# Weighted values in one run, and layer 1 in steps of two key chunks: a two-layer gated cross-attention kernel on one core

## The reference, cut to what matters

```python
x = x + tanh(g_xattn[0]) * L0_xattn(layernorm(x), ctx, ctx)      # two softmaxes, a1 - lam * a2
x = x + tanh(g_ffn[0]) * L0_ffn(layernorm(x))
x = x + tanh(g_xattn[1]) * L1_xattn(layernorm(x), ctx, ctx, mask)
x = x + tanh(g_ffn[1]) * L1_ffn(layernorm(x))
# in either attention, for every batch row and head:
scores = q @ k.T / sqrt(hd);  out = softmax(scores) @ v
```

## Time and profile before

| | us |
|---|---|
| median of 3 runs (2351.14 to 2353.91) | 2351.37 |
| the profiled execution, its own time | 2361.65 |
| its span from first to last instruction | 2359.2 |

### The profile page before, as it was taken

The page is one execution under the profiler, slowest core; times in us unless marked ns, Lnnn a source line. Parts: engine busy times, 40 slices in busy tenths (PEclk is TensorE's granted clock), DMA queues, the critical chain, the costliest instruction groups (busy, mean ns, idle before and its releaser), DMA issues. The chain is left out here.

```text
span 2359.2 us, 67435 instructions
## 1 busy us (share of the span) xinstructions
PE 2192.7 (93%) x27256; PEld 1303.0 (55%) x27256; DVE 1677.1 (71%) x3697; ACT 1507.8 (64%) x2133; POOL 1278.9 (54%) x1418
## 2 busy tenths in 40 slices
PE   4799999999999999999967957999999999999798
PEld 3255555555555555555536843666655666666576
DVE  3688888888888888888816555777766677774644
ACT  2177788777877778778763322767666667766322
POOL 5335655655654554655333445777766777762232
PEclk8599999999999999999997975999999999999699
DMA  3635344344444444444201027667665666661100
GB/s 105 128 77 113 96 98 109 101 94 108 106 97 99 112 96 95 115 93 94 48 7 57 24 61 149 137 142 137 143 131 120 127 144 140 138 126 24 54 1 16
DMA packets 113421, 227.82 MB, mean 97 GB/s; under 512 B 46052, under 2 KB 58596, under 8 KB 112612
## 3 DMA queue, kind: packets, MB, share of 16 engines
q1 hardware_dynamic: 113124, 223.67, 42.8%
HBM read 146.77 MB, written 76.48 MB: 95 GB/s over the span
## 5 line engine op out<-in xcount | busy, mean ns | idle before, releaser
L1061 ACT ACTIVATE probs<-score_ps 125x896 f32<-125x896 f32 x1152 | 1014.3, 915 | 210.3 <-PE score_ps L954 207.9
L1119 DVE TENSOR_REDUCE max_part<-max_ps 112x1 f32<-112x500 f32 x1024 | 654.7, 668 | 115.3 <-PE spare_ps L923 68.3
L970 PE MATMUL acc_ps<-probs,vext 125*32 125x224 f32 (+1 forms) x12288 | 673.2, 316 | 6.6 <-issue 6.1
L923 PE MATMUL max_ps<-kstack,qstack 48*112 48x500 f16 x1535 | 508.1, 405 | 4.9 <-DVE max_part L1119 2.6
L954 PE MATMUL score_ps<-qstack,kstack 50*125 50x224 f16 (+1 forms) x6144 | 454.8, 244 | 17.2 <-ACT probs L1061 13.9
L954 PEld LDWEIGHTS score_ps<-qstack,kstack 50*125 50x125 f16 x6144 | 344.4, 134 | 183.8 <-issue 122.2
L1116 DVE CUSTOM_DVE_ANT_0 kstack<-max_ps,kstack 112x500 f32<-112x500 f32 x511 | 335.3, 675 | 134.2 <-PE max_ps L923 80.1
L1119 DVE TENSOR_REDUCE max_part<-spare_ps 112x1 f32<-112x500 f32 x512 | 343.3, 670 | 64.6 <-PE max_ps L923 63.5
L970 PEld LDWEIGHTS acc_ps<-probs,vext 125*32 125x32 f32 x12288 | 261.7, 109 | 225.8 <-issue 156.5
L923 PE MATMUL spare_ps<-kstack,qstack 48*112 48x500 f16 x769 | 310.7, 404 | 20.2 <-issue 16.9
L923 PEld LDWEIGHTS max_ps<-kstack,qstack 48*112 48x112 f16 x1535 | 173.5, 129 | 143.4 <-issue 77.7
(11 more groups left out here) (200 smaller groups left out, 2697.8 us busy)
## 6 DMA issues: line engine op xcount, KB each, us to landing
kstack<-k_parts SPq DMA_DIRECT2D x384, 187.5 KB, 6.6
k_parts<-khl SPq DMA_DIRECT2D x128, 375.0 KB, 2.8
ctx_f<-in_ctx SPq DMA_DIRECT2D x32, 750.0 KB
ctx_f<-context_parts SPq DMA_DIRECT2D x32, 750.0 KB, 4.4
context_parts<-ctx_f SPq DMA_DIRECT2D x16, 750.0 KB, 3.8
context_parts<-kstack SPq DMA_DIRECT2D x16, 750.0 KB, 3.5
mask_in<-in_mask SPq DMA_DIRECT2D x128, 82.0 KB
qrows<-q_parts SPq DMA_DIRECT2D x384, 7.0 KB, 7.0
```

What stands on the lines that cost most here:

```text
L923: nc.tensor.matmul(room(("P", n, p))[0:PIECE, 0:TK], qstack[n % SLOTS][rows, c, PIECE * i:PIECE * (i + 1)], kstack[n % SLOTS][rows, c, TK ...
L970: last = nc.tensor.matmul(acc_ps[32 * j:32 * j + 32, TT * S * i:TT * S * (i + 1)].rearrange("p (s c) -> p s c", s=S), vext[n % SLOTS][:, t ...
L1061: nc.scalar.activation(probs[t % 2][:, 896 * h:896 * h + 896].rearrange("k (b c) -> k b c", b=2), score_ps[(t * H + h) % 2][0:KT, :, 0:448 ...
L1119: nc.vector.reduce_max(best, scores, AX.X).then_inc(s_red, 1)
```

## The change

Five things change, all in `attend`.

1. `weigh` has no index i: its products follow one another in one run. In layer 0 that is 8 products; before, the search's second pair and the preparation stood between the groups of four (except in step 0).
2. A layer-1 step is now two chunks: `L.steps` is 6 there, `STEPS` replaces `NKT`. A step has two score parts in both layers, in layer 1 one for each chunk, and `weigh` covers both (16 products). `AHEAD` is 3 of 6 steps in layer 1, so the search of row n+2 begins in step 3 of row n; four pieces go in each step.
3. In layer 1 the preparation moves from the search banks to the score banks, and `where` is rewritten: a pair is now (step, bank of the pair). K 0, 1, 2 stand in steps 3, 4, 4, V in 1, 2, 5, M in 3, A in 5, and F is one use of four turned blocks and not two of two.
4. Where the step before had a preparation in the score banks ("crowded"), the second score part stands behind `weigh` (`LATE_SECOND`); otherwise the two parts stand together at the step's head. The first part waits, as layer 0's did, for both exponentials of the step before; a layer-1 chunk waited only for the exponential two chunks back.
5. On SP, in layer 1, `next_context` moves from before `fill_m` to behind `store_k`.

```diff
         keyed = [(kind, i) for kind in "TK" for i in range(NTHIRD)]
     else:
-        where = {("V", 0): (0, 2), ("F", 0): (1, 2), ("V", 1): (2, 2), ("F", 1): (3, 2), ("V", 2): (4, 2), ("K", 0): (5, 2),
-                 ("K", 1): (6, 2), ("M", 0): (7, 2), ("K", 2): (8, 2), ("A", 0): (10, 2)}
+        where = {("F", 0): (1, 1), ("V", 0): (1, 0), ("V", 1): (2, 0), ("M", 0): (3, 1), ("K", 0): (3, 0),
+                 ("K", 1): (4, 0), ("K", 2): (4, 1), ("A", 0): (5, 1), ("V", 2): (5, 0)}
...
-    assert per_step * NKT == L.pieces
-    AHEAD = 5
+    per_step = L.pieces // STEPS
+    assert per_step * STEPS == L.pieces
+    AHEAD = 3 if L.masked else 5
     early = AHEAD * per_step
+    LATE_SECOND = True
```

```diff
@@ -721,8 +718,6 @@
                 if n + 3 < B:
                     load_q(n + 3)
                     next_mask(n + 3)
-                    if L.masked:
-                        next_context(n + 4)
                 if n + 3 < B and not L.masked:
                     next_context(n + 4)
                     store_context(n + 3)
@@ -730,6 +725,8 @@
                     fill_m(n + 1)
                 if n + 3 < B:
                     store_k(n + 3)
+                    if L.masked:
+                        next_context(n + 4)
         s_chain = sem(L.name + "_normalisation_chain")
```

```diff
-                step = n * NKT + t
-                number = step * H + place
+                step = n * STEPS + t
+                number = step * 2 + place
                 h = halves_of(step)[place]
-                if L.masked:
-                    at_least(pe, s_exp, number - 1)
-                elif place == 0:
+                if place == 0:
                     at_least(pe, s_exp, number)
                 else:
...
                     if L.masked:
                         pe.wait_ge(s_big, n + 1)
-                buf = score_ps[(t * H + h) % 2]
-                keys = slice(KT * t, KT * t + KT)
+                buf = score_ps[h]
+                chunk, columns = (t, range(h * 2, h * 2 + 2)) if H == 2 else (2 * t + h, range(PAIRS))
+                keys = slice(KT * chunk, KT * chunk + KT)
...
+            def weigh(n, t):
+
+                pe.wait_ge(s_exp, (n * STEPS + t + 1) * 2)
+                if t == 0:
+                    at_least(pe, s_os, n)
+                    pe.wait_ge(s_v, NTHIRD * (n + 1))
+                chunks = [(t, 0)] if H == 2 else [(2 * t + h, 896 * h) for h in range(2)]
+                for chunk, column in chunks:
+                    for i in range(2):
+                        for j in range(4):
+                            u = 4 * i + j
+                            moving = probs[t % 2][:, column:column + S * 896].rearrange("k (s c) -> k s c", s=S)[:, :, TT * u:TT * u + TT]
+                            last = nc.tensor.matmul(
+                                acc_ps[32 * j:32 * j + 32, TT * S * i:TT * S * (i + 1)].rearrange("p (s c) -> p s c", s=S),
+                                vext[n % SLOTS][:, chunk, u, :], moving, start=(chunk == 0 and i == 0), stop=(chunk == NKT - 1),
+                                skip_group_check=True)
+                last.then_inc(s_av, 1)
```

```diff
-                for t in range(NKT):
+                for t in range(STEPS):
                     weighed = (n, t - 1) if t else (n - 1, LAST)
+                    crowded = n * STEPS + t - 1 in in_scores.values()
                     scores(n, t, 0)
+                    if not crowded:
+                        scores(n, t, 1)
                     search(searched(n, t, 0))
-                    if H == 2:
+                    if crowded and not LATE_SECOND:
                         scores(n, t, 1)
-                    for i in range(2):
-                        if i == 1 and (t or H == 1):
-                            search(searched(n, t, 1))
-                            for user in at_step(n, t, 1):
-                                use(user)
-                        if weighed[0] >= 0:
-                            weigh(*weighed, i)
-                    if t == 0 and H == 2:
-                        search(searched(n, t, 1))
-                    for user in at_step(n, t, 2):
+                    if weighed[0] >= 0:
+                        weigh(*weighed)
+                    if crowded and LATE_SECOND:
+                        scores(n, t, 1)
+                    search(searched(n, t, 1))
+                    for user in at_step(n, t):
                         use(user)
```

```diff
+                    dst, part = (turned[:, i, :], spare_ps[0:SQ, :]) if H == 2 else (
+                        turned[:, :, 0:256], spare_ps[0:SQ, :].rearrange("q (i x) -> q i x", i=2))
+                    nc.scalar.activation(dst, part, ACT.Copy).then_inc(s_turned, 1)
```

More of the change, by code:

```diff
@@ L63, in __init__ @@
         self.o_cols = self.cols // 4
-        self.uses_f = 2
+        self.uses_f = self.halves
+        self.steps = NKT if self.halves == 2 else NKT // 2
 L0 = Layer("L0", 32, 4, False)
@@ L575, in attend, with at_step @@
     LEAD = {"T": 3, "K": 3, "V": 2, "M": 1, "F": -1, "A": -1}
-    def at_step(n, t, side):
-        return [(kind, n + LEAD[kind], i) for (kind, i), place in where.items()
-                if place == (t, side) and 0 <= n + LEAD[kind] < B]
+    def at_step(n, t):
+        return [(kind, n + LEAD[kind], i) for (kind, i), (step, _) in where.items()
+                if step == t and 0 <= n + LEAD[kind] < B]
     def searched(n, t, k):
-        if 2 * k >= per_step:
-            return []
-        d, place = (1, early + t * per_step) if t < NKT - AHEAD else (2, (t - NKT + AHEAD) * per_step)
+        d, place = (1, early + t * per_step) if t < STEPS - AHEAD else (2, (t - STEPS + AHEAD) * per_step)
         return [("P", n + d, place + 2 * k + r) for r in range(2)] if n + d < B else []
@@ L592, in attend @@
     for n in range(B):
-        for t in range(NKT):
-            middle, last = at_step(n, t, 1), at_step(n, t, 2)
-            spare_uses += middle + last
-            if H == 2:
-                in_scores.update({user: n * NKT + t for user in middle})
-                middle = []
-            order += searched(n, t, 0) + middle + searched(n, t, 1) + last
+        for t in range(STEPS):
+            spare_uses += at_step(n, t)
+            in_scores.update({user: n * STEPS + t for user in at_step(n, t)})
+            order += searched(n, t, 0) + searched(n, t, 1)
     order += [(kind, B - 1, i) for kind, i in turnaround]
@@ L904, in use @@
                     pe.wait_ge(s_os, n + 1)
-                    for b in range(2 * S):
-                        k = (i * 2 * S + b) * SQ
+                    for b in range(4):
+                        k = (i * 4 + b) * SQ
                         last = nc.tensor.transpose(spare_ps[0:SQ, 128 * b:128 * b + 128], out_sb[:, k:k + SQ], ident[:, :])
@@ L949, in scores @@
                                          big_eye[HALF * r:HALF * r + SQ, :], start=True, stop=False, skip_group_check=True)
-                here = PAIRS // H
-                for k in range(here):
+                for k, c in enumerate(columns):
                     for r in range(2):
                         rows = slice(HALF * r, HALF * r + KROWS + 2)
-                        last = nc.tensor.matmul(buf[0:KT, r, GC * k:GC * (k + 1)], kstack[n % SLOTS][rows, h * here + k, keys],
-                                                qstack[n % SLOTS][rows, h * here + k, :], start=not L.masked, stop=True,
+                        last = nc.tensor.matmul(buf[0:KT, r, GC * k:GC * (k + 1)], kstack[n % SLOTS][rows, c, keys],
+                                                qstack[n % SLOTS][rows, c, :], start=not L.masked, stop=True,
@@ L1070, in _ @@
             for n in range(B):
-                for t in range(NKT):
-                    for h in range(H):
-                        exps(n, t, h)
+                for t in range(STEPS):
+                    for place in range(2):
+                        exps(n, t, place)
                     if t == 0 and n:
                         copy_output(n)
-                    for user in at_step(n, t, 1) + at_step(n, t, 2):
+                    for user in at_step(n, t):
                         drain(user)
@@ L1150, in _ @@
             for n in range(B):
-                for t in range(NKT):
+                for t in range(STEPS):
                     for user in searched(n, t, 0):
                         reduce_piece(user)
-                    for user in at_step(n, t, 1):
-                        drain(user)
-                    if t == where["F", 1][0] + 1 and n:
+                    if t == where["F", L.uses_f - 1][0] + 1 and n:
                         reciprocals(n)
```

57 lines of the change are left out of this document (19 added, 38 removed).

## The result

The changed kernel takes **2452.56 us** (median; 2446.73 to 2465.94) against 2352.64 us before: 4.3% slower, ratio 1.0429, 95% interval 1.0377 to 1.048. The forecast was 2445. The profiled execution took 2446.73 us, with a span of 2444.9 (2359.2 before).

A forecast was written before the change was run, and what follows sets the result against it. TensorE's order was taken to bound the kernel, and after the change the keys' circle in layer 1. From 2361.65 us, -24 + 110 + 2 gave 2450, taken as 2445; its own range 2400 to 2495, for all 2335 to 2500.

The forecast's parts named there:

- Layer 0, -24 us: In layer 0's attention, a row was to take 34.2 us against 35.01, -24 us over 29 rows.
- The chain that was said to set the step: In layer 0, late second scores, their exponential, then the next step's first scores: a step lasts at least 2.84 us.
- TensorE alone, 21.0: In layer 1, a row whose keys come in time was to take 21.0 us, 1.3 less than before.
- The circle, 23.6: In layer 1, from a row's first search piece through key projection, split, store and fill to the next: 23.6 us.
- X to S: In layer 1, from the first search piece (X) to the end of GpSimd's last key split (S): 10.4 us.
- The context ahead of the fill, 1.6: In layer 1, the context's load stands before the keys' fill in SP's order and delays it: 1.6 us, 0 to 2.5.
- The slow clock, 1.6: In layer 1, TensorE's wait for the fill brings its clock down: 1.6 us a circle, 0 to 2.9.
- The mean: In layer 1, the circle with context and slow clock was to last 26.8 us a row, +110 us over 29 rows.
- S to the next X: In layer 1, from the last key split's end to the next first search piece: 13.2 us and 1.6 for the context.
- the +88 of the sum: Whole kernel against the profiled execution before: -24 in layer 0, +110 in layer 1, +2 for the last rows.

The follow-up runs named there:

- repaired kernel: The changed kernel with layer 1's keys half a step earlier, the context's load ahead of the maxima's fill, and the search half a step later: 2322.87 us.
- experiment 5: The changed kernel with eighteen products that nobody reads before each row's first search piece in layer 1: 2439.86 us.
- experiment 4: The changed kernel with layer 1's context load behind the fill and the queries, one turn of the loop later: 2437.48 us.
- the first edit of experiment 6: The changed kernel with layer 1's key projections half a step earlier in TensorE's order, the context's load not moved: 2477.22 us.

## Why the prediction was right

- **Layer 0, -24 us.** Right: 34.11 a row for 34.2, and -23 us by itself. The chain that was said to set the step also gives 3.66 for the 3.67 of the kernel without the run. The prediction did not see that, with the preparation at the step's end, the late second part also hides the read-out of the bank; without that the row is 36.71.
- **TensorE alone, 21.0.** Right: 20.79 with a small fill, 21.0 in the repaired kernel.
- **The circle, 23.6.** Right in kind, shown by taking out the fill's bytes (wait gone) and by moving either end. With the clock up X to S is 10.37 (experiment 5). The terms that the prediction lists add up to 10.3, not to the 10.4 that it writes.
- **The context ahead of the fill, 1.6.** Right: the fill lands at S + 14.7 in the median for 14.8, and at S + 13.1 with the context behind it (13.2 predicted). The two share the queue: in 1595.5 to 1598 and 1598.5 to 1603 the DMA share was 0.96 and 1.06, at 292 and 226 GB/s, where the fill alone moves 111. By the rule of the Trainium skill that the prediction named (DMA: Bandwidth & Descriptors, Queues, rings and completion order) a ring is consumed in ring order. The trace agrees, with a fill that comes later by the load ahead of it. Sharing the bandwidth without any order could delay it too, and no run here tells the two apart.
- **The slow clock, 1.6.** Somewhat small: X to S is 12.5 for 10.37 with the clock up, so 2.1. The stall that the prediction read as 2.2 us stands as 1.98 in the earlier trace rows.
- **The mean.** 26.65 for 26.8, and here luck had a part: X to S is half a us longer than the 12.0 counted, S to the next X half a us shorter on average than 14.8. The stretch grew by 105 for 110.
- **The rest.** From layer 0's stretch to layer 1's are 350.0 us, 344.7 before. Of these 5 us, 3.4 lie in layer 0's last three rows and belong to its change, which the forecast had counted for the rows of the stretch alone. Between the profiled executions the time grew by 85 us for the +88 of the sum; between the medians it grew by 100.

## What to carry to other kernels

When one engine is full, look not only at its own work but at the circle of anything that is made in one row and used in a later one: make, store, load, use, and the distance in program order back to the next making. A change of order that shortens the engine's work can lengthen that circle, and the row is the longer of the two. A user and its load move together: the keys moved alone cost 25 us, with the load they gained 119. And a wait that brings the clock down costs more than itself.

## What the runs showed that was not expected

- A wait of 1.13 us on TensorE left its clock at 1.00 and the row at 22.1; one of 2.28 or 2.87 us brought it to 0.93 and 0.87 on the row's average and the row to 24.8 and 26.5. Rows of both kinds follow each other in one execution; that a late row makes the next keys late would explain it, but was not tested.
- The clock can fall without one long wait. In the kernel with late second scores and no run, layer 0 had no wait over some 1.0 us in these two rows, and yet:

```profile
210.80:255.30 44.50, 40.50 (x403) 17.73 (x403) 29.72 (x51) 27.62 (x39) 19.74 (x29) 0.96 0.35 80
255.30:308.70 53.40, 51.43 (x403) 20.79 (x403) 30.31 (x51) 28.47 (x40) 19.78 (x29) 0.68 0.29 67
```

- Stalls of TensorE that the profile puts down to "issue", 1 to 4 us long and often in the middle of a run of equal instructions, stand in layer 1 of nine of the twelve traces. There is none in the kernel with a third of the fill, but none either in two kernels with the full fill, those of experiment 4 and of the first edit of experiment 6. What causes them was not tested.
